# Attention stages: the queue on which the byte tables of one-hots are loaded

## The chip, the cores and the metric

The kernel runs on one core of one Trainium2 chip. The metric is the time on the device of one execution, in microseconds, as the median of several runs. A core has TensorE (matrix products), VectorE, ScalarE (ACT), GpSimd (POOL) and SyncE (SP), each with its own stream of instructions; they wait for one another on semaphores. Transfers are issued by an engine into a queue and are moved by 16 DMA engines that all queues share.

## The reference, cut to what matters

A graph of 3125 nodes and 53,125 edges, sorted by target, passes through four graph layers with float32 features of width 256: a weighted convolution with an MLP, a plain convolution, three rounds of typed attention with a dense part behind each, and an attention over edge features. The change touches the attention over edges alone, which in the typed layer is, for each of three rounds:

```python
q_dst = Q[dst]
kt = _typed_transform(K[src], W_E[l], edge_type)
scores = jnp.sum(q_dst * kt, axis=-1) / scale
scores = scores * mu[l].T[edge_type]
m = jax.ops.segment_max(scores, dst, num_segments=N)
e = jnp.exp(scores - m[dst])
s = jax.ops.segment_sum(e, dst, num_segments=N)
w = e / (s[dst] + 1e-10)
agg = jax.ops.segment_sum(V[src] * w[..., None], dst, num_segments=N)
```

The last layer has the same shape (scores, a maximum, exponentials and a sum for each target node), with a score that is the sum of one that was gathered and of a product of the target's features with a code of the edge.

## The kernel before

Edges are laid out in 464 tiles (`NT`) of 128 edges. The targets of one tile lie in one block of 128 nodes, so a 128 x 128 one-hot matrix tells which node of its block each edge belongs to. These matrices are made once and kept in DRAM as bytes, straight (`hot_rows`) and turned (`turned_rows`).

`attend` (L1399) is one attention stage. It is called four times: for the three typed rounds, `L2a0` to `L2a2` in the code and `L2a` in the trace (L3026), and for the last layer, `L3a` (L3071). It walks over the tiles in 29 groups (`WG`) of 16 tiles (`WT`), and a group in 4 quads (`WQ`) of 4 tiles. So one stage has 116 quads and 464 gathers.

For a quad, in the order of the data:

- GpSimd issues 4 gathers (L1460), each of 128 rows of the source table by index, 2 KB a row in the typed stages and 1056 bytes in the last, into one place of a ring of 10 quads (`RQ`; 11 in the last stage). It waits first until VectorE has weighed the quad that had the place before (`weighted_ready`, L50 is the wait itself). In the typed stages three of the ten places are cut from a buffer called `hold`, so the trace lists gathers with two names.
- ScalarE widens the turned bytes of the quad to float32 (`turn`, L1709), and TensorE multiplies them with a block of queries, so that each edge has its target's query (`ask`, L1754).
- VectorE multiplies the query with the gathered keys, or in the last stage with a code loaded from DRAM (`product`, L1513), and sums over each head (`reduce`, L1519).
- When a group's 16 tiles have scores, a chain of small steps finds the maximum of each node over all tiles up to there (L1774 flatten, L1550 and L1555 scans, L1779 sequence, L1566 and L1572, L1784 expand, L1584 to L1604, which writes `zz`), and ScalarE takes the exponent (`soften`, L1729).
- VectorE weighs the gathered values (`weigh`, L1615). ScalarE widens the straight bytes (`widen`, L1717), TensorE sums over the edges of each node (`total`, L1765), and VectorE adds this to the accumulators (`add`, L1544).

The order on each engine is written out by hand. In iteration n of the main loop, the first half of group n's scores is made, then group n - 1 goes through its chain and is weighed, with the second half of group n's products in between. ScalarE's order in iteration n, with m = n - 1, is `widen(m, 1)`, `turn(n + 1, 0)`, `drop(m)`, `turn(n + 1, 1)`, `soften(m)`, `widen(m, 2)`, `turn(n + 1, 2)`, `widen(m, 3)`, `turn(n + 1, 3)`, `widen(n, 0)`.

SyncE loads what is not gathered. For each group these are the turned bytes of 16 tiles (L1470, 256 KB, two buffers `turn8`), the straight bytes (L1475, 256 KB, two buffers `hot8`), the masks for the chain (L1482, 256 KB, and L1484, 4 KB), and in the last stage 4 code tables (L1491, 512 KB each). `load_turn(n)` waits until the bytes of group n - 2 are turned, `load_hot(n)` until those of group n - 2 are widened, `load_pens(n)` for `zz` of group n - 2. GpSimd issues nothing but gathers in these stages.

Of the kernel before, what the change touches and what calls it, by code (L numbers as in the profile page):

```python
# [11 lines left out]
P = 128  # L12
# [20 lines left out]
WT = 16  # L33
WP, WQ, WG = WT // 2, WT // 4, NT // WT
# [9 lines left out]
def wait(eng, sem, value):  # L44

    if isinstance(value, int) and value <= 0:
        return
    eng.wait_ge(sem, value)  # L50
    if not isinstance(value, int):
        eng.nop(nofuse=True)
# [9 lines left out]
def spread(ap, axis, count):  # L62

    shape = list(ap.shape)
    shape.insert(axis, count)
    return ap.unsqueeze(axis).broadcast_to(shape)
# [1332 lines left out]
def attend(nc, c, name, table, width, values, typed, spare=()):  # L1399
# [9 lines left out]
    with Stage(nc, name) as st:  # L1409
        ring = RQ if typed else 11  # L1410
        rows = list(spare) + [st.sb(f"rows{s}", [P, 4, width])[:, :, :] for s in range(ring - len(spare))]
        turn8 = [st.sb(f"turn8_{k}", [P, WT * P], U8) for k in range(2)]
        hot8 = [st.sb(f"hot8_{k}", [P, WT * P], U8) for k in range(2)]
# [20 lines left out]
        if not typed:  # L1434
# [4 lines left out]
        turn_landed, hot_landed, pens_landed = (  # L1439
            [st.sem(f"{x}_landed{k}") for k in range(2)] for x in ("turn", "hot", "pens"))  # L1440
# [12 lines left out]

        @block.gpsimd
        def _(pool):
            for n in range(WG * WQ):
                wait(pool, weighted_ready, n - ring + 1)
                for u in range(4):
                    t = n * 4 + u
                    pool.indirect_dma_start(rows[n % ring][:, u, :], None, table,  # L1460
                                            bass.IndirectOffsetOnAxis(ap=index_of[:, t:t + 1], axis=0)
                                            ).then_inc(landed[n % ring], 16)
            for s in range(ring):
                pool.wait_ge(landed[s], 64 * len(range(s, WG * WQ, ring)))

        @block.sync
        def _(sp):
            def load_turn(n):
                wait(sp, turned_ready, (n - 1) * WQ)
                sp.dma_start(turn8[n % 2][:, :], c.turned_rows[:, n * WT * P:(n + 1) * WT * P]  # L1470
                             ).then_inc(turn_landed[n % 2], 16)

            def load_hot(n):
                wait(sp, hot_ready, (n - 1) * WQ)
                sp.dma_start(hot8[n % 2][:, :], c.hot_rows[:, n * WT * P:(n + 1) * WT * P]  # L1475
                             ).then_inc(hot_landed[n % 2], 16)

            def load_pens(n):
                wait(sp, zz_ready, n - 1)
                wait(sp, shrink_ready, n - 2)  # L1480
                own = c.mask_rows[n * WT:(n + 1) * WT, 0:4 * P]
                sp.dma_start(pens[n % 2][:, :, :].rearrange("p k e -> p (k e)"), spread(own, 1, H)  # L1482
                             ).then_inc(pens_landed[n % 2], 16)
                sp.dma_start(first_hot[n % 2][:, :], c.mask_rows[n * WT:n * WT + 1, 4 * P:5 * P].broadcast_to([H, P])  # L1484
                             ).then_inc(pens_landed[n % 2], 16)

            def load_codes(n):
                if not typed:
                    for q in range(n * WQ, (n + 1) * WQ):
                        wait(sp, multiplied, q - codes + 1)  # L1490
                        sp.dma_start(code[q % codes][:, :, :], c.code_rows[:, 4 * q:4 * q + 4, :]  # L1491
                                     ).then_inc(code_landed[q % codes], 16)

            load_turn(0)
            for n in range(WG):
                load_codes(n)
                if n + 1 < WG:
                    load_turn(n + 1)
                load_pens(n)
                load_hot(n)  # L1500

        @block.vector
        def _(dve):
# [1601 lines left out]
```

## Time and profile before

| | |
|---|---|
| median of 3 runs | 5544.4 us (5542.47 to 5549.68) |
| span of the profiled execution | 6456.7 us |
| TensorE matmuls, busy | 4457.4 us (69%) |
| weight loads, busy | 3493.0 us (54%) |
| VectorE, busy | 3832.0 us (59%) |
| ScalarE, busy | 1605.5 us (25%) |
| GpSimd, busy | 3364.1 us (52%) |
| queue 0, written by GpSimd | 549.90 MB, 34.1% of the 16 DMA engines |
| queue 1, SyncE's | 404.92 MB, 19.6% of the 16 DMA engines |
| mean granted clock of TensorE | 0.831 |

The profiled execution is an execution of its own; besides its span, no time of it is given. In a line of the trace, `L1460 POOL` is work of GpSimd that line 1460 issues, `a<-b,c` says what is written and read, buffer numbers left out. Where idle time is shown, the name behind the arrow is what ended it: "issue" means nothing that the profile shows, "remote" an event that it can't assign. A semaphore's number is used again in later stages, so that a DMA of an earlier stage is sometimes named as the releaser.

### The profile page before, as it was taken

Reading aid. Unit: us, or ns where it says so; the run is one execution under the profiler, and the core shown is the slowest. Engines: PE = TensorE matmul, PEld = TensorE weight load, DVE = VectorE, ACT = ScalarE, POOL = GpSimd, SP = SyncE. Lnnn points to the kernel's source line nnn. Section 1 sums busy time; section 2 is a strip of 40 time slices with the busy share of each in tenths; the row PEclk is TensorE's granted clock in tenths of the full one; section 3 lists DMA queues with packets and bytes.
Section 4 is the critical chain, followed back from the end, with each engine's and each line's share of the span. In section 5 each row is a group of like instructions: output and inputs, shape, how many; then the busy total and the mean of one; then the engine's idle time right before and its main releaser. Section 6 shows DMA issues by size and latency. Waiting matters only on the chain. (4 is left out here: it accounts for less than half of the span.)

```text
span 6456.7 us, 68859 instructions
## 1 busy us (share of the span) xinstructions
PE 4457.4 (69%) x19341; PEld 3493.0 (54%) x19341; DVE 3832.0 (59%) x8692; ACT 1605.5 (25%) x3882; POOL 3364.1 (52%) x3108
## 2 busy tenths in 40 slices
PE   5666664577766666778857767796766679766776
PEld 4455453444436455557845555685555558545554
DVE  7544443544455666675347766643766776567777
ACT  3433332200004111113421211243211214312221
POOL 2588886366644555541356555134555530256663
PEclk9888887788888778779977777898778779878887
DMA  3688887255556555542266556315556541256664
GB/s 139 121 124 125 121 125 150 81 184 184 182 165 208 168 173 181 181 144 58 81 189 182 174 175 181 89 56 165 169 175 182 176 147 39 80 168 183 195 192 134
DMA packets 508435, 959.75 MB, mean 149 GB/s; under 512 B 85846, under 2 KB 298020, under 8 KB 507251
## 3 DMA queue, kind: packets, MB, share of 16 engines
q0 software_dynamic: 224512, 549.90, 34.1%
q1 hardware_dynamic: 283426, 404.92, 19.6%
q8 instruction: 170, 2.79, 0.2%
q14 instruction: 199, 1.62, 0.1%
q10 hardware_dynamic: 128, 0.52, 0.0%
HBM read 718.56 MB, written 236.50 MB: 148 GB/s over the span
## 5 line engine op out<-in xcount | busy, mean ns | idle before, releaser
L1460 POOL DMA_INDIRECT L2a_rows<-kv_rows,typed_index x960 | 966.3, 1007 | 627.8 <-DVE L2a_weighted L1615 349.9
L1765 PE MATMUL L2a_sums<-L2a_weighted,L2a_hot 128*128 128x264 f32 x2784 | 830.5, 450 | 166.8 <-DVE L2a_weighted L1615 159.4
L1754 PE MATMUL L2a_query<-x,L2a_turned 128*128 x2784 | 819.8, 447 | 55.8 <-ACT L2a_turned L1709 33.0
L867 POOL DMA_INDIRECT sum_rows<-L0s_rows,L0s_row_of x464 | 724.6, 1562 | 152.9 <-issue 119.4
L1765 PEld LDWEIGHTS L2a_sums<-L2a_weighted,L2a_hot 128*128 128x128 f32 x2784 | 591.2, 221 | 314.5 <-DVE L2a_weighted L1615 186.2
L1754 PEld LDWEIGHTS L2a_query<-x,L2a_turned 128*128 128x128 f32 x2784 | 627.2, 229 | 181.4 <-issue 62.5
L1460 POOL DMA_INDIRECT hold<-kv_rows,typed_index x432 | 445.4, 1031 | 449.8 <-DVE L2a_weighted L1615 279.5
L1460 POOL DMA_INDIRECT L3a_rows<-feature_rows,index x464 | 489.1, 1054 | 301.7 <-DVE L3a_weighted L1615 155.1
L1285 POOL DMA_INDIRECT L1s_rows<-rows,index x464 | 451.0, 972 | 351.2 <-issue 133.8
L1717 ACT ACTIVATE L2a_hot<-L2a_hot 128x512 f32<-128x512 uint8 x348 | 218.7, 629 | 1470.8 <-PE L2a_sums L1765 726.6
L1002 PE MATMUL L0s_message<-features,L0s_share 128*128 x928 | 312.8, 496 | 285.9 <-ACT L0s_share L967 285.9
L2296 POOL TENSOR_SCALAR L2d_here<-hold,mask 128x256 f32<-128x256 f32 x200 | 183.1, 933 | 552.6 <-DVE hold L2372 404.5
L1342 PE MATMUL L1s_code_ps<-L1s_wide,L1s_fields 128*128 128x512 f32 x464 | 285.8, 702 | 219.3 <-DVE L1s_code L1311 138.4
L1519 DVE TENSOR_REDUCE L2a_score<-L2a_prods 128x32 f32<-128x1024 f32 x348 | 417.8, 1201 | 0.4
L1002 PEld LDWEIGHTS L0s_message<-features,L0s_share 128*128 128x128 f32 x928 | 215.3, 242 | 364.9 <-issue 329.1
L1765 PE MATMUL L3a_sums<-L3a_weighted,L3a_hot 128*128 128x264 f32 x928 | 282.7, 457 | 92.6 <-DVE L3a_weighted L1615 89.3
L1709 ACT ACTIVATE L2a_turned<-L2a_turn 128x512 f32<-128x512 uint8 x348 | 216.9, 624 | 507.7 <-PE L2a_query L1754 191.8
L1513 DVE TENSOR_TENSOR L2a_prods<-L2a_query,L2a_rows 128x1024 f32<-128x1024 f32 x240 | 291.9, 1216 | 76.5 <-remote 47.3
L901 DVE TENSOR_TENSOR L0s_hot<-count,early 128x512 f32<-128x512 f32 x116 | 80.5, 694 | 419.0 <-ACT L0s_hot L980 412.7
L1305 DVE TENSOR_TENSOR acc<-acc,L1s_sums 128x256 f32 x232 | 97.4, 420 | 378.4 <-remote 176.5
L1544 DVE TENSOR_TENSOR acc<-acc,L2a_sums 128x264 f32 x696 | 290.4, 417 | 10.8 <-PE L2a_sums L1765 9.1
L1615 DVE TENSOR_TENSOR L2a_weighted<-L2a_rows,L2a_weighted 128x1024 f32<-128x1024 f32 x240 | 292.4, 1218 | 3.4 <-ACT L2a_weighted L1729 1.3
(428 smaller groups left out, 8550.9 us busy)
## 6 DMA issues: line engine op xcount, KB each, us to landing
code_rows<-L1s_code SPq DMA_DIRECT2D x116, 512.0 KB
L3a_code<-code_rows SPq DMA_DIRECT2D x116, 512.0 KB
L0s_wide<-source_rows SPq DMA_DIRECT2D x116, 256.0 KB
L2a_turn<-turned_rows SPq DMA_DIRECT2D x87, 256.0 KB
L2a_pens<-mask_rows SPq DMA_DIRECT2D x87, 256.0 KB
L2a_hot<-hot_rows SPq DMA_DIRECT2D x87, 256.0 KB
kv_rows<-L2d_key_rows SPq DMA_DIRECT2D x50, 384.0 KB, 2.6
kv_rows<-L2d_value_rows SPq DMA_DIRECT2D x150, 128.0 KB, 2.4
```

What stands on the lines that cost most here:

```text
L867: pool.indirect_dma_start(c.sum_rows[u], bass.IndirectOffsetOnAxis(ap=row_of[:, 4 * n + u:4 * n + u + 1], axis=0), rows[n % ring][:, u, :] ...
L1002: last = pe.matmul(message[n % 2][:, u, :], share[n % 2][:, u, :], at(c.q, b[i])[:, 0:D], start=True, stop=True)
L1285: pool.indirect_dma_start(rows[n % ring][:, u, :], None, table, bass.IndirectOffsetOnAxis(ap=c.index[:, t:t + 1], axis=0)).then_inc(landed ...
L1342: pe.matmul(code_ps[j % 2][:, :, :].rearrange("p k d -> p (k d)"), fields[g % 2][:, :], wide[:, 2 * j % FT:2 * j % FT + 2, :].rearrange("p ...
L1460: pool.indirect_dma_start(rows[n % ring][:, u, :], None, table, bass.IndirectOffsetOnAxis(ap=index_of[:, t:t + 1], axis=0)).then_inc(lande ...
L1513: dve.tensor_tensor(prods[q % 2][:, :, :], query[q % 2][:, :, :], other, ALU.mult).then_inc(multiplied, 1)
L1519: last = dve.tensor_reduce(own.rearrange("p k h -> p (k h)"), prods[q % 2][:, :, :].rearrange("p k (h d) -> p (k h) d", h=H), AX.X, ALU.add)
L1544: dve.tensor_tensor(at(c.acc, b), at(c.acc, b), sums[(m * WP + j) % held][:, :], ALU.add).then_inc(added, 1)
L1615: dve.tensor_tensor(weighted[:, 4 * q:4 * q + 4, :].rearrange("p k (h d) -> p k h d", h=H)[:, :, :, 0:HD], rows[quad % ring][:, :, values: ...
L1717: act.activation(hot[quad % 2][:, :, :].rearrange("p u e -> p (u e)"), hot8[m % 2][:, q * 4 * P:(q + 1) * 4 * P], ACT.Copy).then_inc(hot_r ...
L1754: last = pe.matmul(query[q % 2][:, u, :], turned[quad % 2][:, u, :], at(c.q, b[2 * q + u // 2]), start=True, stop=True)
L1765: last = pe.matmul(sums[(m * WP + j) % held][:, :], hot[quad % 2][:, j % 2 * 2 + k, :], weighted[:, 2 * j + k, :], start=k == 0, stop=k == 1)
```

## The change

The loads of the turned and of the straight byte tables move from SyncE's program into GpSimd's. The first turned table is issued ahead of the first gather. The straight table of group n - 1 is issued behind the gathers of the second quad of group n, the turned table of group n + 1 behind those of its fourth quad, and the last straight table behind the last gather. What each load waits for, its size, its buffers and the semaphore that tells of its landing stay as they were. SyncE keeps the codes and the masks.

```diff
         @block.gpsimd
         def _(pool):
+            def load_turn(n):
+                if n < WG:
+                    wait(pool, turned_ready, (n - 1) * WQ)
+                    pool.dma_start(turn8[n % 2][:, :], c.turned_rows[:, n * WT * P:(n + 1) * WT * P]
+                                   ).then_inc(turn_landed[n % 2], 16)
+
+            def load_hot(n):
+                if 0 <= n < WG:
+                    wait(pool, hot_ready, (n - 1) * WQ)
+                    pool.dma_start(hot8[n % 2][:, :], c.hot_rows[:, n * WT * P:(n + 1) * WT * P]
+                                   ).then_inc(hot_landed[n % 2], 16)
+
+            load_turn(0)
             for n in range(WG * WQ):
                 wait(pool, weighted_ready, n - ring + 1)
                 for u in range(4):
...
+                if n % WQ == 1:
+                    load_hot(n // WQ - 1)
+                if n % WQ == 3:
+                    load_turn(n // WQ + 1)
+            load_hot(WG - 1)
             for s in range(ring):
                 pool.wait_ge(landed[s], 64 * len(range(s, WG * WQ, ring)))
 
         @block.sync
         def _(sp):
-            def load_turn(n):
-                wait(sp, turned_ready, (n - 1) * WQ)
-                sp.dma_start(turn8[n % 2][:, :], c.turned_rows[:, n * WT * P:(n + 1) * WT * P]
-                             ).then_inc(turn_landed[n % 2], 16)
-
-            def load_hot(n):
-                wait(sp, hot_ready, (n - 1) * WQ)
-                sp.dma_start(hot8[n % 2][:, :], c.hot_rows[:, n * WT * P:(n + 1) * WT * P]
-                             ).then_inc(hot_landed[n % 2], 16)
-
...
-            load_turn(0)
             for n in range(WG):
                 load_codes(n)
-                if n + 1 < WG:
-                    load_turn(n + 1)
                 load_pens(n)
-                load_hot(n)
```

## Rows read from the trace of the kernel before

**Rows 1.** Busy time by stretch, whole stages; columns in the first line.
```profile
core 0: us, PE busy (x) PEld busy (x) DVE busy (x) ACT busy (x) POOL busy (x), PEclk, DMA share, GB/s
2064.00:2920.00 856.00, 576.24 (x2096) 444.64 (x2097) 579.55 (x965) 160.65 (x292) 470.64 (x464) 0.79 0.57 172
3262.00:4120.00 858.00, 577.46 (x2094) 445.64 (x2095) 579.93 (x965) 160.54 (x292) 470.77 (x464) 0.77 0.57 171
4460.00:5316.00 856.00, 573.02 (x2090) 441.93 (x2090) 578.09 (x964) 160.67 (x292) 470.26 (x464) 0.78 0.57 171
5610.00:6456.00 846.00, 549.94 (x2086) 427.58 (x2086) 605.20 (x1112) 161.79 (x290) 489.13 (x464) 0.80 0.59 178
```

**Rows 2.** The same view, one group in mid-stage and the first stage's last full group.
```profile
2834.60:2862.90 28.30, 21.26 (x72) 16.32 (x72) 19.62 (x34) 5.15 (x11) 16.30 (x16) 0.74 0.56 167
2862.90:2883.00 20.10, 18.00 (x70) 14.48 (x71) 19.43 (x34) 4.84 (x9) 8.72 (x8) 0.80 0.44 131
```

**Rows 3.** Timeline of GpSimd: start, duration, work, idle time before and what ended it.
```profile
2837.89 0.94 POOL L1460 DMA_INDIRECT hold<-kv_rows,typed_index  x1 [7.16 <-DVE L2a_weighted L1615]
2839.14 1.90 POOL L1460 DMA_INDIRECT hold<-kv_rows,typed_index  x1 [0.31 <-issue]
2841.35 0.95 POOL L1460 DMA_INDIRECT hold<-kv_rows,typed_index  x1 [0.30 <-issue]
2842.60 1.05 POOL L1460 DMA_INDIRECT hold<-kv_rows,typed_index  x1 [0.30 <-issue]
...
2857.82 0.95 POOL L1460 DMA_INDIRECT L2a_rows<-kv_rows,typed_index  x1 [0.30 <-issue]
2866.21 0.94 POOL L1460 DMA_INDIRECT L2a_rows<-kv_rows,typed_index  x1 [7.44 <-DVE L2a_weighted L1615]
...
2876.12 0.94 POOL L1460 DMA_INDIRECT L2a_rows<-kv_rows,typed_index  x1 [0.30 <-issue]
```

**Rows 4.** Timeline of all engines in mid-stage, the rows around one hole.
```profile
2399.91 0.23 PE L1779 MATMUL L2a_small<-L2a_ends,head 128*8 128x32 f32 x2
...
2407.84 0.27 DVE L1566 TENSOR_TENSOR_SCAN L2a_up<-links,L2a_up,L2a_small 8x32 f32<-8x32 f32 x1 [6.74 <-issue]
...
2408.64 0.63 PE L1784 MATMUL L2a_small<-L2a_tops,heads 8*128 8x32 f32 x2 [5.67 <-issue]
```

**Rows 5.** Timeline of VectorE at the end of the first attention stage.
```profile
2910.88 0.43 DVE L1544 TENSOR_TENSOR acc<-acc,L2a_sums 128x264 f32 x1 [0.46 <-PE L2a_sums L1765]
2911.63 0.20 DVE L2314 TENSOR_SCALAR L2d_total<-acc 128x40 f32<-128x40 f32 x1 [0.32 <-PEq L87]
```

**Rows 6.** Timeline of SyncE's queue in one group.
```profile
2413.57 0.53 SPq L1482 DMA_DIRECT2D L2a_pens<-mask_rows  x1
2414.15 0.49 SPq L1484 DMA_DIRECT2D L2a_first_hot<-mask_rows  x1
2423.50 0.33 SPq L1475 DMA_DIRECT2D L2a_hot<-hot_rows  x1
2425.22 0.32 SPq L1470 DMA_DIRECT2D L2a_turn<-turned_rows  x1
```

**Rows 7.** The instructions on the turned table, and waits that its landing ended.
```profile
L1709 ACT ACTIVATE L2a_turned<-L2a_turn x348: 612/629/632, 2066.6 to 5272.7; 128x512 f32<-128x512 uint8 x174
  DMA L2a_turn<-turned_rows: 21.8, 3
  DMA L3a_turn<-turned_rows: 7.0, 1
```

**Rows 8.** Direct loads issued by GpSimd elsewhere: five in the timeline, and all 56.
```profile
99.71 2.77 POOL L303 DMA_DIRECT2D raw<-edge_rows  x5
L303 POOL DMA_DIRECT2D raw<-edge_rows x56: 484/484/750, 88.4 to 124.1; - x56
```

**Rows 9.** Timelines of VectorE and of SyncE's queue at the first attention stage's start.
```profile
2105.72 1.23 DVE L1513 TENSOR_TENSOR L2a_prods<-L2a_query,L2a_rows 128x1024 f32<-128x1024 f32 x1 [15.69 <-DMA x<-x_in]
2121.16 0.42 DVE L1550 TENSOR_TENSOR_SCAN L2a_climb<-L2a_pens,L2a_small 128x128 f32<-128x128 f32 x1 [14.21 <-remote]
2075.64 0.33 SPq L1475 DMA_DIRECT2D L2a_hot<-hot_rows  x1
2121.84 0.32 SPq L1470 DMA_DIRECT2D L2a_turn<-turned_rows  x1
```

## The prediction

> **What bounds the kernel now.** I first set the times beside the profile: 5544.4 us is the median of the runs shown, the profiled execution spans 6456.7 us, 912.3 us more. No time of that execution is shown besides its span, so the sum below is a difference, added to the median; whether the profile's waits exist in the timed runs is the main question. Then I cut the span into its stages [rows 1]. The change touches the four attention stages, 856, 858, 856 and 846 us, 3416 us together. Each walks through 29 groups of 16 tiles.
>
> In one steady group, 28.3 us long [rows 2], no compute engine is full: VectorE 19.62 us, TensorE 21.26, GpSimd 16.30 for 16 gathers. GpSimd's figure hides its issue gaps: one gather starts 1.25 us after the other, 0.95 busy and 0.30 between [rows 3]. So the queue of the gathers needs 16.30 + 16 x 0.30 = 21.1 us per group, and then waits 7.44 us (28.3 in all) for VectorE to free a place of the ring [rows 3]. Read as it stands, the profile has 7 us of slack on GpSimd in each group.
>
> But the 28.3 us are no work. VectorE stands idle for 6.74 us before L1566 in mid-group; that instruction waits for the two small matmuls of L1779, which the trace places at 2399.91, eight microseconds earlier. After it TensorE's L1784 starts 5.67 us after its last work [rows 4]. These holes sit in nearly every group and nothing that is computed fills them. The next row is what decides for me: the group from 2862.90 to 2883.00 does the same work for VectorE (19.43 us, 34 instructions) and nearly all of TensorE's (70 instructions against 72), but GpSimd issues only its last 8 gathers in it, and it takes 20.1 us, not 28.3 [rows 2]. VectorE is then full. TensorE's granted clock, a mean over stretches at 1.2 and 2.4 GHz, is 0.74 in the one and 0.80 in the other, no difference that could make 8 us. So a group without the holes is VectorE's 20.1 us, and the gathers' queue with its 21.1 us is longer than that.
>
> Do the timed runs have the holes? A stage without them would be bound by GpSimd. For the typed stages: 16.30 us per 16 gathers gives 1.02 + 0.30 = 1.32 us a gather, 464 of them 612 us; with an estimated 38 us for the first landing and for the last group and its tail (the last gather of the first stage is issued at 2876.12 and the next stage's first work of VectorE is at 2911.63 [rows 3, 5]) 650 us against 857, thus 207 x 3 = 620. For the last stage 489.13 us over 464 gathers [rows 1] is 1.054, with 0.30 thus 1.354 us each, 628 + 34 = 662 against 846, thus 184; its group is 21.7 us for GpSimd and 605.20 / 29 = 20.9 for VectorE. Together 804 us of the 912 us by which the span exceeds the median; the idle time in the other loops has room for the remaining 108. This agreement is why I take the timed runs to be bound by the queue of the gathers in all four stages.
>
> **The change part by part.**
> *Taken off SyncE:* per group one load of the turned and one of the straight table, 256 KB each, 0.32 and 0.33 us of issue [rows 6]. SyncE is idle nearly always: in a group it issues four transfers. What remains in its queue, the masks, goes out at the same events as before, since those wait for zz and shrink. In the last stage the code tables no longer have a table load behind them. Who waited for the two loads? ACT for the turned table, 21.8 us in 3 waits, one at the start of each typed stage, and 7.0 in one wait in the last [rows 7]; nobody for the straight one. Worth zero, since the first load is still needed at the start.
>
> *Put on GpSimd:* 29 + 29 loads in each of four stages, 232 in all. The trace has no such load on this queue. Nearest rows: the 56 direct loads of L303 on GpSimd, five of which take 2.77 us, so one every 0.57 us (0.484 + 0.09), each of one row cut into 16 pieces of 512 B [rows 8]; and the gathers, 128 rows of up to 2 KB, one every 1.25 us, 1.32 with the stretched ones [rows 3]. The load has 128 rows like a gather, and no index to read like the direct one. A cost under 0.57 has no reason, as 16 pieces already cost that. So 0.57 to 1.32 us each; I take 0.95, the middle, since it is like the one in its rows and like the other in its form. Sum: 232 x 0.95 = 220 us, between 132 and 306. All of it lies on the path if the gathers' queue is the bound: 21.1 + 2 x 0.95 = 23.0 us per group against 20.1 for VectorE.
>
> *The waits before them.* A gather of quad k waits until quad k - 10 is weighed (11 in the last stage), so the queue runs ahead. The straight table n - 1 goes out behind quad 4n + 1 and waits for the widening of group n - 3; the turned table n + 1 behind quad 4n + 3 and waits for the turning of group n - 1, two iterations of the loop back. When the queue is late rather than early, both have long happened. Were one to hold, all later gathers stand behind it, and VectorE's products after these; I price it at nothing because the gathers before it waited for something later.
>
> *Where the data comes later.* If the queue has no lead, the turned table for group n + 1 lands some 3 us after the gathers of group n. ACT reads it ahead of the softmax of group n - 1, so that softmax comes later in the group than now; what follows it up to the same point of the next group is, as an estimate, VectorE's 20.1 us and the two turnings of 0.63 us that ACT does first [rows 2, 7], 21.4 us, still under 23.0. Cover is 1.6 us per group; if it were gone, each microsecond beyond it costs 116.
>
> *At a stage's start* the first turned table goes ahead of the first gather: included in the 232. ACT's wait grows by as much as that issue.
>
> What the Trainium skill says against the change: "SBUF — State Buffer", section "SBUF: two separate sides", has it that a DMA issued by GpSimd has its descriptors written by GpSimd, which is locked out while VectorE runs an operation through both ports. Here one gather in each group takes 1.90 us instead of 0.95 [rows 3], and the trace does not show for which operation. It is a rival below.
>
> **The rivals.**
> *Hidden (0.18).* The holes are in the timed runs too, and GpSimd keeps its 7 us of slack per group [rows 3]. Then 2 x 0.95 us go into the slack, the ring keeps its lead, and only the start of each stage moves, 1 us x 4: 5548 us, 5540 to 5556. For it: the profile as it stands. Against it: the 912 us, which then must come out of the 3040 us of the other stages. The Trainium skill, "DMA: Bandwidth & Descriptors", section "Issuing engines are not separate DMA queues", says that the choice of the issuing engine saves only issue time, usually small beside the transfer; by it alone this is the outcome.
>
> *Partly bound (0.12).* Timed groups last 22 us rather than 21.1, so 0.9 of the 1.9 us is hidden: 116 x 1.0 = 116 us, 5660.
>
> *Stretched loads (0.05).* Each load meets what stretches one gather per group: 1.90 + 0.30 us each, 232 x 2.2 = 510 us, 6054. Against: the gathers around the stretched one take 0.94 to 1.05 us [rows 3].
>
> *Faster (0.08).* TensorE's holes appear where a full set of gathers runs beside SyncE's tables and vanish in the last groups. If they stem from two queues at once, a rest of them is in the timed runs, and taking two of SyncE's three large transfers per group away shortens them. Half a microsecond of 8.2 per group gives 116 x 0.5 = 58 us, 5486. It decides only where the gathers' queue has more slack than the 1.9 us put on it, thus from 23.0 us a group. Against: holes of 14 and 15 us stand in the first stage's start, where SyncE has nothing to load [rows 9].
>
> **How the numbers follow.** Forecast: GpSimd-bound, 5544.4 + 220 = 5765 us, 5676 to 5850 by the bounds of one load, chance 0.57. The likeliest case gives the number. The range reaches down over the partly bound and the hidden cases to 5540 and up to 5850; left out are the faster case, the stretched one and a few hundredths beside, 0.17 in all. Slower by over 0.2% (11 us, about what a measurement of this kernel can tell from no change): 0.57 + 0.12 + 0.05 and 0.01 of the hidden case, 0.75. Within it: 0.17. Faster: 0.08.
>
> **What would show it.** In the changed kernel's profile: 232 direct loads on GpSimd between those of L1460, start to start of the next gather 0.6 to 1.3 us; GpSimd's wait for the weighted rows down from 7.4 to about 5.5 us a group; and, as the holes belong to the profiled execution, a span hardly longer than 6456.7 us though the timed runs are 4% slower. If span and median move alike, the holes are real and my reading of the 912 us is wrong. If GpSimd's slack per group shrinks by 4 us, the loads are stretched. If ACT begins to wait for the turned table in mid-stage, the lateness costs, not the issue. The prediction is most likely wrong in the size of one load, and in whether the timed runs' groups are shorter than 23 us.

## The result and the profile after

The changed kernel takes 5758.6 us (5757.28 to 5762.61), the kernel before 5547.0 us beside it (5542.47 to 5551.92): a ratio of 1.038, 95% interval 1.0365 to 1.0394, 211.5 us slower. The forecast was 5765.

The page of the changed kernel, its span and its two large queues:

```profile
span 5755.6 us, 68859 instructions
...
PE 4272.7 (74%) x19341; PEld 3387.6 (59%) x19341; DVE 3825.6 (66%) x8692; ACT 1609.2 (28%) x3882; POOL 3526.3 (61%) x3340
...
q0 software_dynamic: 243072, 610.73, 42.2%
q1 hardware_dynamic: 250018, 344.09, 18.8%
```

Here the span is the timed time. The 6456.7 us of the profile ahead of the prediction belonged to that one execution: profiled anew, the unchanged kernel spans 5547.1 us, and no other profile of this study has its holes. What made them stays open. The two profiled executions of before and after differ by 208.5 us, the medians by 211.5. From here on, "before" is this second profile.

Its attention stages, and then those of the changed kernel [rows 1]; the columns are the stretch, its length, the busy time and number of instructions of PE, PEld, DVE, ACT and POOL, TensorE's clock, DMA share, GB/s:

```profile
1971.40:2605.20 633.80, 512.52 (x2086) 394.78 (x2086) 565.43 (x956) 165.99 (x290) 465.06 (x464) 0.93 0.76 229
4875.00:5523.80 648.80, 526.06 (x2086) 405.64 (x2086) 585.05 (x1100) 163.61 (x290) 485.09 (x464) 0.90 0.74 226
```

```profile
1974.10:2655.90 681.80, 531.52 (x2086) 416.73 (x2086) 569.63 (x955) 161.04 (x290) 509.91 (x522) 0.87 0.72 213
5024.40:5731.90 707.50, 537.59 (x2086) 419.11 (x2086) 587.05 (x1100) 160.89 (x290) 533.02 (x522) 0.85 0.70 208
```

VectorE's work is the same; GpSimd has 58 instructions more in each stage, and the stage is 48 to 59 us longer. GpSimd by line, first before and then after; behind the bar stand busy time, mean ns of one, and the idle time before:

```profile
L1460 POOL DMA_INDIRECT L2a_rows<-kv_rows,typed_index x960 | 959.4, 999 | 292.5 <-issue 292.5
L1460 POOL DMA_INDIRECT hold<-kv_rows,typed_index x432 | 433.0, 1002 | 179.9 <-issue 179.9
```

```profile
L1473 POOL DMA_INDIRECT L2a_rows<-kv_rows,typed_index x960 | 979.4, 1020 | 292.5 <-issue 292.2 <-DVE L2a_weighted L1619 0.3
L1473 POOL DMA_INDIRECT hold<-kv_rows,typed_index x432 | 445.1, 1030 | 131.6 <-issue 131.0 <-DVE L2a_weighted L1619 0.6
L1459 POOL DMA_DIRECT2D L2a_turn<-turned_rows x87 | 52.2, 600 | 48.6 <-issue 48.5
L1465 POOL DMA_DIRECT2D L2a_hot<-hot_rows x87 | 52.1, 598 | 0.1
```

```profile
L1460 POOL DMA_INDIRECT L3a_rows<-feature_rows,index x464 | 485.1, 1045 | 154.4 <-issue 154.4
L1473 POOL DMA_INDIRECT L3a_rows<-feature_rows,index x464 | 498.5, 1074 | 141.4 <-issue 141.1 <-DVE L3a_weighted L1619 0.3
```

The last two rows are the last stage, before and after. In neither kernel does a gather wait for VectorE beyond the usual 0.3 us (in [rows 3] it did, 7 us a group). GpSimd goes from one issue to the next throughout: it bounds all four stages before the change. Two things are new: the loads, 0.60 us each, and gathers that last 20 to 30 ns more on average.

GpSimd's timeline after, in mid-stage, around one load of each kind; start, duration, work, idle time before:

```profile
2306.38 0.95 POOL L1473 DMA_INDIRECT L2a_rows<-kv_rows,typed_index  x1 [0.30 <-issue]
2307.63 0.94 POOL L1473 DMA_INDIRECT L2a_rows<-kv_rows,typed_index  x1 [0.30 <-issue]
2308.57 0.60 POOL L1459 DMA_DIRECT2D L2a_turn<-turned_rows  x1
2309.47 0.97 POOL L1473 DMA_INDIRECT hold<-kv_rows,typed_index  x1 [0.30 <-issue]
...
2319.37 0.60 POOL L1465 DMA_DIRECT2D L2a_hot<-hot_rows  x1
2320.27 0.98 POOL L1473 DMA_INDIRECT hold<-kv_rows,typed_index  x1 [0.30 <-DVE L2a_weighted L1619]
2321.56 1.78 POOL L1473 DMA_INDIRECT hold<-kv_rows,typed_index  x1 [0.31 <-issue]
```

From 2307.63 to 2309.47 are 1.84 us, where two gathers without a load between them stand 1.25 apart: a load takes 0.59 us of the queue. For all 232 that is 137 us. Of these, 224 lie between two gathers of a stage; there the next gather starts 0.90 us after the end of the last one on average and not 0.30, so these loads lengthen the queues by 134 us. Four go ahead of a stage's first gather and four behind its last. That leaves some 75 of the 211.5 us unexplained.

To see where they are, I cut each stage into the *queue* (start of the first gather to start of the last) and the *end* (from there to the end of the last add). For the first stage before, queue and end come from these rows, 2576.65 being the last gather:

```profile
2576.65 0.95 POOL L1460 DMA_INDIRECT L2a_rows<-kv_rows,typed_index  x1 [0.30 <-issue]
...
2604.45 0.43 DVE L1544 TENSOR_TENSOR acc<-acc,L2a_sums 128x264 f32 x1 [0.46 <-PE L2a_sums L1765]
```

and after from these, an end of 31.9 us instead of 28.2:

```profile
2623.92 0.95 POOL L1473 DMA_INDIRECT L2a_rows<-kv_rows,typed_index  x1 [0.30 <-issue]
...
2655.41 0.43 DVE L1548 TENSOR_TENSOR acc<-acc,L2a_sums 128x264 f32 x1 [0.46 <-PE L2a_sums L1769]
```

Summed over the four stages, in us. *Stretch* is what the stages' 1856 gathers are busy beyond 0.946 us each, their median:

```
                    queue    ends   first gather later   stretch of gathers
before             2438.0   108.7            -             121.7
after              2617.5   131.7            2.8           167.2
difference         +179.5   +23.0           +2.8           +45.5
```

134 us of issue and 45.5 of stretch are the 179.5 by which the queues grew. With the ends and the starts it is 205 us in the stages; 2.3 us more stand ahead of the first stage, 208 of the 208.5 together. TensorE's mean granted clock is also lower, 0.884 against 0.906, but in the queues the two terms leave nothing for it. The experiments ask what the stretch and the ends come from.

### The profile page after: what moved, and what is told of

Same layout as the page of the kernel before. It is cut to its first block and busy times, and to the rows that moved or that the text cites. A ratio compares the mean times of both kernels' runs of the same rounds, so it can differ in the third digit from the quotient of the medians.

```text
span 5755.6 us, 68859 instructions
## 1 busy us (share of the span) xinstructions
PE 4272.7 (74%) x19341; PEld 3387.6 (59%) x19341; DVE 3825.6 (66%) x8692; ACT 1609.2 (28%) x3882; POOL 3526.3 (61%) x3340
## 5 line engine op out<-in xcount | busy, mean ns | idle before, releaser
L1473 POOL DMA_INDIRECT L2a_rows<-kv_rows,typed_index x960 | 979.4, 1020 | 292.5 <-issue 292.2
L1758 PE MATMUL L2a_query<-x,L2a_turned 128*128 x2784 | 721.8, 406 | 63.2 <-ACT L2a_turned L1713 34.8
L1758 PEld LDWEIGHTS L2a_query<-x,L2a_turned 128*128 128x128 f32 x2784 | 570.7, 208 | 165.6 <-issue 67.1
L1353 PE MATMUL L1s_sums<-L1s_rows,L1s_hot 128*128 128x256 f32 x928 | 256.5, 401 | 130.2 <-issue 108.1
L1353 PEld LDWEIGHTS L1s_sums<-L1s_rows,L1s_hot 128*128 128x128 f32 x928 | 175.6, 198 | 292.1 <-issue 226.2
```

Source lines behind the costliest of these rows:

```text
L1353: last = pe.matmul(sums[j % held][:, 0:D], hot[n % hots_held][:, u, :], rows[n % ring][:, u, :], start=k == 0, stop=k == 1)
L1758: last = pe.matmul(query[q % 2][:, u, :], turned[quad % 2][:, u, :], at(c.q, b[2 * q + u // 2]), start=True, stop=True)
```

## The experiments

Each ratio is to the kernel before, timed beside it (medians 5550.2 to 5558.6 us).

**Before, profiled again.** The unchanged kernel; no edit.

> The kernel before, unchanged, profiled once more. Theory Q (the queue of the gathers bounds the attention stages): a profile without the holes shows a span near 5545 us, groups of 21.1 us, and GpSimd waiting for weighted rows under 0.5 us a group. Rival H (the holes of the first profile are part of the kernel): the span is near 6450 us again and groups last 28 us. Rival S (there is slack on GpSimd and the groups are bound by something else): span near 5545 us, groups of 21 to 23 us, and GpSimd still waits 1 us or more a group for weighted rows.

5548.69 us, span 5547.1, the rows above. It settles the first question of the prediction: typed groups of 20.8 to 21.0 us on average, not 28.3, and GpSimd never idle in them but for its issue gaps.

**The issue alone.** SyncE keeps its two loads; GpSimd issues spare loads of 128 rows of 64 bytes in the places of the change.

```diff
+        unused = st.sb("unused", [P, UN], U8)
+        spared = st.sem("spared")
...
+                pool.dma_start(unused[:, :], c.turned_rows[:, 0:UN]).then_inc(spared, 16)
...
+                if n % WQ == 3 and n // WQ + 1 < WG:
+                    pool.wait_ge(spared, 16 * made[0])
+                    spare_load()
```

> The kernel before, with SyncE still loading both tables, but GpSimd issues 58 loads more in each attention stage, at the places where the change puts them: 128 rows of 64 bytes each into a buffer that nobody reads, so issue cost without the bytes and without any table being late. In the changed kernel a gather starts 1.84 us after the one before it where a load lies between, 1.25 us elsewhere, so a load costs 0.59 us of the queue, 232 of them 137 us. Theory Q: 5547 + 137 = 5684 us (ratio 1.025). Theory L (the 212 us come from the turned table's landing late, for which ACT waits): 5547 us (1.000). Both together, Q for 137 and L for the remaining 75: 1.025 here.

5698.6 us, 1.0266 (1.0249 to 1.0283): 148 of the 211 us, without any real load moved. Queues +141.8, of which stretch +8.4; ends 108.0, as before. The rest stands mostly ahead of the first stage, which starts 8.6 us later. So a load costs its issue even when nobody waits for what it brings.

**The lateness alone.** SyncE issues everything as before, but the turned table n + 1 also waits until the gathers of quad 4n + 2 have landed.

```diff
                 wait(sp, turned_ready, (n - 1) * WQ)
+                if n:
+                    own = n * WQ - 2
+                    wait(sp, landed[own % ring], 64 * (own // ring + 1))
```

> The kernel before, SyncE issues everything, but the load of the turned table of group n + 1 waits also until the gathers of the third quad of group n have landed, which is about when the changed kernel issues it. Lateness without issue cost on GpSimd. Theory Q: 5547 us, within 0.3%. Theory L: the whole of the loss, 5758 us (1.038). Q for 137 us and L for the remaining 75: 5622 us (1.013).

5564.1 us, 1.0027 (1.0016 to 1.0039). The ends grow by 18.9 us, to 127.6, the queues shrink by 10.1 and the stretch by 10.1. So a late turned table lengthens each stage's end by some 5 us, while its mid-stage waits are hidden behind the gathers' queue. (The table is somewhat less late here than in the change: ScalarE waits 394.5 us for it in all, there 592.6.)

**Each half of the change.** Both edits are shown against the changed kernel. Only the turned loads on GpSimd:

```diff
-            def load_hot(n):
-                if 0 <= n < WG:
-                    wait(pool, hot_ready, (n - 1) * WQ)
...
-                if n % WQ == 1:
-                    load_hot(n // WQ - 1)
...
                 load_pens(n)
+                load_hot(n)
```

> One half of the change: only the turned table's load goes to GpSimd, the straight one's stays with SyncE. Theory Q: 116 loads of 0.59 us, 5547 + 68 = 5615 us (1.012). Theory L: all of the loss, 5758 us (1.038), since the turned table is the one that ACT waits for. Q and L together: 68 + 75, 5690 us (1.026).

5632.5 us, 1.0152 (1.0135 to 1.0169): between the 5615 of issue alone and the 5690 of both together. And only the straight loads there:

```diff
-            load_turn(0)
             for n in range(WG * WQ):
...
-                if n % WQ == 3:
-                    load_turn(n // WQ + 1)
...
+            load_turn(0)
             for n in range(WG):
                 load_codes(n)
+                if n + 1 < WG:
+                    load_turn(n + 1)
```

> The other half of the change: only the straight table's load goes to GpSimd. Theory Q, issue alone: 116 loads of 0.59 us, 5549 + 68 = 5617 us (ratio 1.012). If the two halves add up to the whole: 212 - 82 = 130 us, 5679 us (1.023). If the half of the straight table costs its 68 us only, the whole is more than its halves, and some 60 us come from both being there.

5626.4 us, 1.0137 (1.0115 to 1.0158). The halves give 82 and 76, 158 us together, not 211: the costs don't add. The turned half adds 29.3 us to the ends, the straight one 2.1. In the queues the turned half has 67 of issue (112 loads between two gathers) and 24.5 of stretch *less*, +42.1 measured; the straight half 67 and 3.2 less, +63.2 measured. In the straight half ScalarE waits 617 us in all for the straight table's bytes, and neither the queues nor the ends show it.

**The turned table early.** The change, with `load_turn(n + 1)` behind quad 4n and not 4n + 3.

```diff
-                if n % WQ == 3:
+                if n % WQ == 0:
                     load_turn(n // WQ + 1)
```

> The changed kernel with the turned table of group n + 1 issued behind the gathers of the first quad of group n, not of the fourth: the same loads, one of them 15 us sooner. In the changed kernel each stage ends 3.3 to 11 us later behind its last gather than in the kernel before, 23 us in all. Theory Q (issue only): 5758 us, ratio 1.038. Theory L for the tail: the 23 us come back, 5735 us, 1.034. If lateness is also what stretches the gathers by another 37 us: 5698 us, 1.027.

5695.8 us, 1.0258 (1.024 to 1.0277): 62.8 us less than the change, with the same 232 loads. The ends are 106.9 us again, the stretch 133.9 (of the profiled execution, which at 5709.6 us was the slowest of the four). One line takes back most of what isn't issue. ScalarE's wait does not vanish: it goes over to the straight table, 594 us in 111 waits, and costs nothing there.

**The size of the load.** The spare loads with rows of 2 KB, 256 KB in all like the tables.

```diff
-UN = 64
+UN = 2048
```

> As e2_spare_loads, but each of the 58 spare loads a stage moves the whole 256 KB of a table (128 rows of 2 KB) and not 8 KB, with SyncE's own loads kept. Theory Q, cost by the instruction: as with 64 bytes a row, 5698 us, 1.027. Rival B (the bytes on the gathers' queue stretch the gathers): the changed kernel's stretch of 45 us instead of 8 comes with it, 5735 us or more, 1.034.

5704.0 us, 1.0275 (1.0254 to 1.0295). A load of 32 times the bytes takes the same 0.60 us, and the kernel 5 us more, inside the intervals.

```profile
L1460 POOL DMA_DIRECT2D L2a_unused<-turned_rows x174 | 104.0, 598 | 47.9 <-issue 47.7
```

```profile
L1460 POOL DMA_DIRECT2D L2a_unused<-turned_rows x174 | 104.2, 599 | 46.7 <-issue 46.4
```

(First the 64-byte rows, then the 2 KB rows; the real loads take 596 to 600 ns on average.)

**What stretches a gather.** In the kernel before, 122 gathers last over 1.2 us, the longest 2.0, and each of them overlaps a weighing of VectorE (L1615). The timeline shows one:

```profile
2303.11 0.94 POOL L1460 DMA_INDIRECT L2a_rows<-kv_rows,typed_index  x1 [0.30 <-issue]
2303.99 1.21 DVE L1615 TENSOR_TENSOR L2a_weighted<-L2a_rows,L2a_weighted 128x1024 f32<-128x1024 f32 x1
2304.35 1.67 POOL L1460 DMA_INDIRECT L2a_rows<-kv_rows,typed_index  x1 [0.30 <-issue]
2306.33 0.95 POOL L1460 DMA_INDIRECT L2a_rows<-kv_rows,typed_index  x1 [0.30 <-issue]
```

The weighing reads two operands from SBUF, the gathered values and the probabilities. VectorE's product (L1513) is as long, 1.2 us, but its query is in PSUM, and no gather is held by it: 168 gathers start in the first 0.8 us of a product, and their stretch is 0.1 us in all. 115 gathers start in the first 0.8 us of a weighing; their stretch is 82 us, and the median of them ends 0.82 us after the weighing does. So I moved one operand of the weighing: ScalarE also writes the exponents to PSUM, and the weighing reads them there. The first form gives them a bank of their own, and for that the buffers of sums go from three to two.

```diff
-    held, codes = 3, 4
+    held, codes = 2, 4
...
+        small, probs = st.ps("small", [P, 512]), st.ps("probs", [P, 512])
...
-                    weighted[:, 4 * q:4 * q + 4, HD::HC].unsqueeze(3).broadcast_to([P, 4, H, HD]), ALU.mult
+                    probs[:, 4 * q * H:4 * (q + 1) * H].rearrange("p (k h) -> p k h", h=H)
+                    .unsqueeze(3).broadcast_to([P, 4, H, HD]), ALU.mult
...
+                    act.activation(probs[:, 0:P], below_ps, ACT.Exp).then_inc(prob_ready, 1)
```

> The kernel before, but the exponents that the weighing multiplies with are also written into a PSUM bank of their own, and VectorE's weighing reads them there, so it has one input in SBUF instead of two; to free the bank, TensorE's sums have two buffers, not three. In the clean profile of the kernel before, all 122 gathers of over 1.2 us overlap a weighing. Theory W (an operation with two inputs in SBUF holds GpSimd up): the gathers' 122 us over their shortest time fall to under 30 and, since VectorE's own 20.1 us a group binds then, the time falls by about 0.9 us a group, 5549 - 100 = 5449 us, 0.982. Rival (any work of VectorE does, or the DMA rings do): the gathers stay as long, 5549 us, 1.000. If the two buffers of sums bind, it is slower than 1.000 with short gathers.

```profile
L1460 POOL DMA_INDIRECT L2a_rows<-kv_rows,typed_index x960 | 910.6, 949 | 357.1 <-issue 263.6 <-DVE L2a_weighted L1615 93.5
L1460 POOL DMA_INDIRECT hold<-kv_rows,typed_index x432 | 409.4, 948 | 220.4 <-issue 166.6 <-DVE L2a_weighted L1615 53.7
```

No gather lasts over 1.2 us any more, the stretch is 3.7 us and not 121.7, though 224 gathers still start in the first 0.8 us of a weighing: the cause is shown. But the kernel takes 5665.3 us, 1.0203 (1.0182 to 1.0224), and now the gathers wait for VectorE: the idle time before them is 64.6 and 40.5 us more than before. Something else had become the bound.

**The lost buffer alone.** The kernel before with `held` 2 and nothing more.

```diff
-    held, codes = 3, 4
+    held, codes = 2, 4
```

> The kernel before with two buffers of sums instead of three and nothing else, as a control for e8b_probs_bank. If the two buffers made e8b slow: 5640 us or more, 1.016. If it was the second exponent: 5550 us, 1.000.

5673.9 us, 1.0228 (1.0181 to 1.0275), typed groups of 21.3 to 21.4 us on average, queues +32.2, stretch 121.8, ends 167.0 instead of 108.7. The lost buffer of sums, not the operand in PSUM, made the form above slow.

**The operand in PSUM, with all buffers.** The exponents go into the unused quarter of the bank `small`. TensorE writes this bank for the next group, so its flatten waits until the group before is weighed.

```diff
+        probs_ps = small[:, 3 * P:4 * P]
...
+                    probs_ps[:, 4 * q * H:4 * (q + 1) * H].rearrange("p (k h) -> p k h", h=H)
+                    .unsqueeze(3).broadcast_to([P, 4, H, HD]), ALU.mult
...
+                    act.activation(probs_ps, below_ps, ACT.Exp).then_inc(prob_ready, 1)
...
+                wait(pe, weighted_ready, n * WQ)
```

> The kernel before with three buffers of sums, the exponents also written into a free part of the PSUM bank of the small products, and read there by VectorE's weighing; TensorE's flattening of the next group waits in addition until the group's four quads are weighed. No gather should be stretched: their excess over 0.946 us falls from 122 us to under 10. Theory Q with VectorE as the next bound (20.1 us a typed group, 20.9 in the last stage): 0.9 us x 116 saved, 5550 - 100 = 5450 us, 0.982. Rival: the longer wait of TensorE or ScalarE's second exponent binds as in e8b, whose groups took 21.6 us: 5600 us or more, 1.010, with groups above 21 us and GpSimd waiting for weighted rows.

```profile
L1461 POOL DMA_INDIRECT L2a_rows<-kv_rows,typed_index x960 | 911.3, 949 | 292.6 <-issue 290.7 <-DVE L2a_weighted L1616 1.8
L1461 POOL DMA_INDIRECT hold<-kv_rows,typed_index x432 | 409.5, 948 | 176.2 <-issue 175.3 <-DVE L2a_weighted L1616 0.9
```

5461.8 us, 0.9839 (0.9823 to 0.9856): the fastest kernel of the study, and faster than both. Its queues are 2322.1 us, 115.9 less than before; the stretch went from 121.7 to 5.7, 116.0 less. The weighing takes 1.21 us as before. The kernel gains less than its queues, 88.6 us: the ends are 15.9 us longer (TensorE's new wait may be why; no run shows it), and the first stage starts 10.8 us later.

**The change upon this.** The same edit in the changed kernel, and then with the turned table early as well.

> The changed kernel with the exponents read from PSUM as in e9, so that nothing stretches its gathers. The changed kernel's queue is made of 1.25 us for a gather, 0.59 for a load and 167 us of stretch. Theory Q: without stretch a group's queue is 16 x 1.25 + 2 x 0.59 = 21.2 us, 5758 - 167 = 5591 us, 1.007 against the kernel before. If the turned table's lateness binds by itself, whatever the queue does: above 5650 us, 1.018.

> The kernel of e11 (the change, with the exponents read from PSUM) with the turned table issued behind the first quad of a group as in e6b. Theory Q for what is left: the queue stays at 615 us a stage, 35 us over e9's 580.5, since 58 loads of 0.59 us are 34 us; the ends of the stages, 33 to 37 us behind the last gather in e11, go back to the 30 us of e9: about 17 us less than e11, 5602 us, 1.009. If lateness of the turned table costs nothing once there is no stretch: 5619 us, 1.012.

5619.1 us, 1.012 (1.0103 to 1.0137), and 5593.0, 1.0064 (1.0046 to 1.0083). The first came out between the two values expected: the stretch is gone, the ends are not. The second stands 131 us above the fastest kernel. Its queues are 136.6 us longer, 3.1 of them stretch, and its ends 7.8 shorter (116.8 against 124.6): 133.5 us is the cost of issue by itself, 0.60 us for each of the 224 loads between two gathers. Between the first and the second lie 26 us, of which 24.2 are in the ends (141.0 against 116.8): without the stretch, the late table costs the ends and nothing else.

The whole queue in one rule, 0.60 us for each load between two gathers plus the difference in stretch, against what was measured (all us, to the kernel before):

```
                       issue   stretch    sum    queues measured
the change              134     +45.5    +180       +179.5
issue alone             134      +8.4    +142       +141.8
spare, 2 KB rows        134     +17.4    +151       +150.2
turned early            134     +12.2    +146       +145.8
turned only              67     -24.5     +43        +42.1
straight only            67      -3.2     +64        +63.2
lateness alone            0     -10.1     -10        -10.1
operand in PSUM           0    -116.0    -116       -115.9
the change upon it      134    -110.8     +23        +23.2
```

It holds to about 1 us in each. The stretch itself follows from where the gathers start: in the first 0.8 us of a weighing start 115 of them before, 182 after the change, 132 with the table early, 104 with lateness alone and 80 in the turned half, and among these five kernels the stretch is larger the more there are (121.7, 167.2, 133.9, 111.6, 97.2 us). What the rule doesn't give is why more of them start there in one kernel than in another; I take it that this shifts with everything that shifts VectorE against the queue, which is argued and not shown. With both loads on the queue the late table had the larger stretch (167.2 against 133.9), with both on SyncE the smaller (111.6 against 121.7), so it isn't a price that one can give to lateness. Each stretch is also that of one execution.

One more thing stays open: ahead of the first attention stage, where no edit touches the code, the kernels differ by up to 17 us (the stage's first row, the clearing of `acc`, starts at 1971.9 before, 1974.2 after, 1982.7 with the operand in PSUM, 1985.0 with the table early, 1988.4 with two buffers of sums). These are single executions, so it may differ from one to the next of the same kernel as well. For the change it is 2.3 us of the 211.5.

## Why the prediction was right, and where it wasn't

*The bound.* Right, and it carried the rest. The prediction took the waits for VectorE in its profile for something that the timed runs don't have, on two grounds: the span was 912.3 us over the median, and one group without holes took 20.1 us, less than the 21.1 us of the gathers' queue. Before's clean profile has groups of 20.9, 21.0, 20.8 and 21.7 us on average against the forecast 21.1 and 21.7, and its four stages are 868 us shorter than in the first profile, of the 912 (forecast 804). The levels of a stage were a little high, 650 and 662 us against 634 and 649; in the typed ones it is 7 us too much of queue, from the 16.30 us of one group with more stretch than the mean, and 10 too much of end (28 us, not 38).

*Taken off SyncE at zero.* Right. With the loads still on SyncE and spares on GpSimd the time was 148 us worse than before, so it is what GpSimd gains that costs. And with the loads gone from SyncE and the table early the time is 5695.8, within 3 us of that: what SyncE loses is worth nothing that shows.

*The size of a load: the term that was mis-sized.* "I take 0.95, the middle": it is 0.59, close to the lower bound of 0.57, which came from loads of one row cut into 16 pieces [rows 8]. 232 x 0.95 = 220 should have been 137, of which 134 are in the queues. The choice of the middle rested on the likeness to a gather in its 128 rows; neither their number nor their length (64 bytes or 2 KB) raised the time in the queue over that of 16 pieces by more than 0.03 us.

*Two terms at zero that weren't.* The prediction had one gather per group stretched to 1.90 us [rows 3] and carried it as a fixed part of the group; it grew by 45.5 us in all. And it priced the later turned table at nothing, with "Cover is 1.6 us per group". In mid-stage this was roughly so: ScalarE did begin to wait for the table's bytes, in most groups:

```profile
ACT L2a_turned L1713 <- DMA L2a_turn<-turned_rows: 429.8, 86, 13.6
ACT L3a_turned L1713 <- DMA L3a_turn<-turned_rows: 162.8, 29, 12.8
```

(Waiter, releaser, us in all, times, the longest; before, 21.7 us in 3 waits in the typed stages, much as in [rows 7], with most of the wait then on TensorE's query.) These are 593 us of wait, of which the time shows little: the queue bounds the group, and ScalarE, busy 28% of the span, has idle time in any case. But behind the last gather of a stage there is no queue to hide in, and there each stage lost 3 to 11 us, 23.0 together. The prediction called such mid-stage waits the sign that "the lateness costs, not the issue"; they were there, and the issue was the larger part all the same, 137 against 63 us that putting the table early gave back.

*The sum.* 220 was forecast and 211.5 measured, but the closeness is partly luck: 83 us too much for the loads stand against 74 that were not in it, 45.5 of stretch, 23.0 of ends and a few us of starts and of the difference between executions. With the right size of a load the method would have said 5681, low by 77. The sign and the bound were reasoned; the third figure was not.

*What would show it.* Wrong in one place: "a span hardly longer than 6456.7 us". The prediction took the holes for a property of profiling. They were of one execution, and the changed kernel's profile has none, nor has the unchanged kernel's second one. The waits "from 7.4 to about 5.5 us a group" could for the same reason not be seen: they were 0 in both.

*The rivals.* Hidden (5548) and partly bound (5660): excluded, no gather waits for a free place before the change. The rule of the Trainium skill that stands beside the first ("DMA: Bandwidth & Descriptors", "Issuing engines are not separate DMA queues") is that the issuing engine decides only issue time, usually small beside the transfer. The runs agree: spares and real loads cost alike, and one turned load is 0.60 us of issue against 3.7 us to its landing. It doesn't follow that the issue is hidden: as the issuing engine was the bound, 224 small times became 134 us of the 5547. Faster (5486): nothing of it. Stretched loads (6054): the loads stay at 573 to 641 ns, none is held, though 86 of them overlap a weighing.

What the prediction asked of this rival, for which operation a gather is held, has its answer now: the weighing with two operands in SBUF. The Trainium skill ("SBUF — State Buffer", "SBUF: two separate sides") tells of a pair of ports that VectorE and GpSimd share under an exclusive lock. The sentence that the prediction drew on is about VectorE's operations in a 2-port mode, during which GpSimd can't write descriptors; were the weighing such an operation, the direct loads would have been held as well, and they were not. The same section also names a VectorE operation with two SBUF inputs, against a GpSimd operation that reads SBUF. The trace agrees with this second one: 116 of 121.7 us go away when one operand leaves SBUF, and the direct loads, which unlike the gathers have no indices to read from SBUF, are not held. That the read of the indices is what is held is argued from this and not shown by a run of its own.

## What to carry to other kernels

Compare a profile's span with the timed median before believing its waits, and find which queue is never idle: there a direct load cost 0.60 us at 8 KB and at 256 KB, while on SyncE it cost nothing that could be measured. Where work comes later behind a bound that hides it in the loop, look at the end of each stage, where nothing hides it. Where GpSimd's issues are the bound, try to keep one operand of VectorE's long products in PSUM, if there is room for it.

## What was not expected of the hardware

- A direct load issued by GpSimd took 0.60 us with 128 rows of 64 bytes and with 128 rows of 2 KB, and was not held by a weighing: of the 64-byte ones 79 started in the first 0.8 us of one, and none took over 0.62. A gather of 128 rows took 0.95, with 0.30 between two.
- A gather's issue beside VectorE's weighing of 128 x 1024 float32 with both inputs in SBUF took up to 2.0 us instead of 0.95; with one input in PSUM none was over 1.2, in 1856, and the weighing itself stayed at 1.21 us. Moving that input made the kernel before 1.6% faster.
- Moving the small operand to PSUM is only a gain if the bank is free: two buffers of sums instead of three cost 2.3%.
